# Two halves of 512 tokens as two streams in a kernel with two attention branches and two layers

## The chip, the cores and the metric

The kernel runs on one core of one Trainium2 chip. The metric is the device time of one launch in microseconds; lower is better. PE is TensorE (matmuls; PEld is its weight loads), DVE is VectorE, ACT is ScalarE, POOL is GpSimd and SP is SyncE, which here issues the DMAs inside the loop. Each engine works through its own list of instructions in the order in which it is written; engines meet only at semaphores.

## What is computed

For each of four batch elements (1024 tokens of 128 features) the input is normalised and given to two branches whose results are added to the input. The first branch, called the group branch here, is one transformer layer with 16 heads of 8 features, 4 key heads and a causal window of 32 tokens. The second is two layers with 8 heads of 64 features and local attention over blocks of 64 tokens.

```python
x = L0_attn_x
xn = _layernorm(x, axis=-1)
x = x + _L0_attn_ref(xn, ...) + _L0_ffn_ref(xn, ...)

# one of the two layers of _L0_ffn_ref
h = shift_token(x)                  # half of the features come from the token before
q, k, v = split(h @ wqkv)
q, k = l2norm(q) * qs, l2norm(k) * ksc
q, k = rotary_xpos(q, k)
o = local_attention(q, k, v)        # block of 64 queries, its block and the one before; masked softmax
x = x + o @ wo
h = shift_token(x)
h = (h - mu) / sqrt(var + 1e-05) * lg + lb
a, g = split(h @ w1 + b1)
x = x + (a * gelu(g)) @ w2 + b2
```

## The kernel before

The four batch elements run one after the other in a loop with a barrier between two. Within one, tokens are handled in two halves of 512 (`c` is 0 or 1, `CH` is 512) and eight tiles of 128 (`t`); data lies with features on partitions and tokens along the row. All is float32. Every engine's order is written out by hand.

The order of one element is: transposes in, projections and attention of the group branch, its output; then for each layer `l` of the second branch the projections of half 0, the projections of half 1, local attention of all eight tiles, and output projection and feed-forward of both halves; then the transposes out. The group branch's own feed-forward (`a_hidden`, `a_output`) stands among the feed-forward of the layers.

*Products* go through a ring of four banks of PSUM: `product(i, ...)` writes bank `i % RING`, where `i` is a use numbered by the table `STAGES`; `taken` waits until a use has been drained.

*A projection tile* (`k` from 0 to 7; four of keys, four of queries) is one product on PE; two copies on ACT out of its bank, `raw` (scaled, L976) and `sq` (squared, L980); two DMAs that SP issues (L452) to write `rot`, which is `raw` with neighbouring rows exchanged; on DVE `pc` = `raw` x table (L1038) and `ps_` = `rot` x table (L1040); and on POOL their sum into `qk` (L494). There are four slots of `raw` and `rot`. The sums of squares (L739), turned by PE, become norms by a chain of small operations on DVE (`norms`, L292 to L1179), which PE turns and spreads (`turn_norms`, L755, `spread_norms`) and DVE multiplies into the key tiles (`scale`, L1188). Values (`vB`, L995) are also needed shifted by 64 tokens: two large DMAs per half write `vS` (L460, L462), issued by SP behind the last exchange of the half.

*Local attention* of a tile has two groups `g` of four heads. PE puts the mask into two banks (L620) and adds 16 products of queries and keys (L628), in which the groups, and with them the upper and lower 64 rows, alternate; DVE takes the maximum of both groups (L1085) and multiplies by the norm (L1087); ACT takes eight exponentials with their sums (L872, each with a read of the accumulator); DVE inverts the sums (L1101, L1107) and scales group 0 (L1103), POOL group 1 (L500); PE turns (L640); DVE copies group 0 to `probT` (L1094) and ACT group 1 (L883); PE weighs the values (L656); ACT copies the heads to `oT` (L889). Scores have two pairs of banks, turned probabilities one bank for each group, heads two banks. The loop runs one tile ahead with scores, one behind with the turn and two behind with the weighing.

*Feed-forward* of a half: output projection (four products into one bank), sum and shift on DVE (L1209, L1131, L1132), centring and mean by products, copies on ACT (L914, L915), the root as Exp(-0.5 x Ln) on ACT (L921, L926), their product on DVE (`hTz<-raw,ps_`, L1127), six hidden products, Gelu on ACT (L1013), the gate on DVE (L1235), three products out and the sum (L1243). On ACT, Ln, Exp and Gelu each need a table load when the one before was another.

## Time and profile before

| | before |
|---|---|
| median of 3 runs | 1451.54 us (1446.1 to 1462.14) |
| profiled execution, its own time | 1459.8 us |
| its span, first to last instruction | 1458.1 us |
| mean granted TensorE clock | 0.877 |
| busy: PE, DVE, ACT, POOL | 77%, 60%, 53%, 20% |

Shares are of the span. The granted clock is a share of full speed: 1.00 is 2.4 GHz and 0.50 is 1.2 GHz, and the rows show no third level. In a timeline row, the number in brackets is how long the engine had been idle before, and what ended that.

### The profile page before, as it was taken

Reading aid. Unit: us, or ns where it says so; the run is one execution under the profiler, and the core shown is the slowest. Engines: PE = TensorE matmul, PEld = TensorE weight load, DVE = VectorE, ACT = ScalarE, POOL = GpSimd, SP = SyncE. Lnnn points to the kernel's source line nnn. Section 1 sums busy time; section 2 is a strip of 40 time slices with the busy share of each in tenths; the row PEclk is TensorE's granted clock in tenths of the full one; section 3 lists DMA queues with packets and bytes.
Section 4 is the critical chain, followed back from the end, with each engine's and each line's share of the span. In section 5 each row is a group of like instructions: output and inputs, shape, how many; then the busy total and the mean of one; then the engine's idle time right before and its main releaser. Section 6 shows DMA issues by size and latency. Waiting matters only on the chain. (4 is left out here: it accounts for less than half of the span.)

```text
span 1458.1 us, 23509 instructions
## 1 busy us (share of the span) xinstructions
PE 1124.0 (77%) x8682; PEld 620.1 (43%) x8754; DVE 878.6 (60%) x1738; ACT 768.9 (53%) x1928; POOL 291.5 (20%) x228
## 2 busy tenths in 40 slices
PE   5986788678698668867869877886787976797677
PEld 4752453154374245325437425432534732542353
DVE  5549655963445865596345596468545467648744
ACT  1355674485235556447523556653942453945574
POOL 1105112410101411241010141033202033204210
PEclk9698899889859879988986988997997796999799
DMA  6003101400101310140010131023001014003100
GB/s 260 1 29 117 27 1 58 112 2 15 31 1 45 101 27 1 58 112 2 15 32 1 51 98 23 1 73 98 2 15 32 1 59 111 2 1 123 48 16 15
DMA packets 39201, 66.22 MB, mean 45 GB/s; under 512 B 5408, under 2 KB 19232, under 8 KB 37152
## 3 DMA queue, kind: packets, MB, share of 16 engines
q1 hardware_dynamic: 37920, 62.43, 14.0%
q10 hardware_dynamic: 1152, 2.10, 0.4%
q8 instruction: 78, 1.28, 0.4%
q14 instruction: 51, 0.42, 0.1%
HBM read 13.12 MB, written 2.10 MB: 10 GB/s over the span
## 5 line engine op out<-in xcount | busy, mean ns | idle before, releaser
L494 POOL TENSOR_TENSOR qk<-pc,ps_ 128x512 f32<-128x512 f32 x128 | 194.3, 1518 | 583.8 <-DVE ps_ L1040 583.8
L872 ACT ACTIVATE prob<-bank,negb,inv_norm 128x128 f32<-128x128 f32 x512 | 233.0, 580 | 57.3 <-DVE negb L1087 57.3
L1040 DVE TENSOR_TENSOR ps_<-rot,tab_s 128x512 f32<-128x512 f32 x128 | 172.5, 1347 | 25.9 <-DMA rot<-raw 25.9
L872 ACT ACTIVATION_READ_ACCUMULATOR prob<-bank,negb,inv_norm 128x1 f32 x512 | 163.3, 328 | 0.0
L510 PE MATMUL bank<-hTz,wb_s 128*128 128x512 f32 x256 | 139.5, 675 | 4.3 <-ACT sq L980 4.3
L1085 DVE TENSOR_REDUCE negb<-bank 128x8 f32<-128x1024 f32 x64 | 78.3, 1223 | 94.5 <-PE bank L628 94.4
L976 ACT ACTIVATE raw<-bank,vec_s 128x512 f32<-128x512 f32 x128 | 90.0, 703 | 81.6 <-PE bank L510 46.5
L500 POOL TENSOR_TENSOR prob<-prob,recb 128x512 f32<-128x512 f32 x64 | 66.7, 1041 | 320.1 <-DVE recb L1107 320.1
L1038 DVE TENSOR_TENSOR pc<-raw,tab_s 128x512 f32<-128x512 f32 x128 | 109.3, 854 | 18.2 <-ACT raw L976 18.1
L656 PE MATMUL bank<-probT,vS 128*64 128x64 f32 x1024 | 67.9, 231 | 38.6 <-issue 34.2
L510 PE MATMUL bank<-hTz,w_s 128*128 128x512 f32 (+1 forms) x192 | 87.8, 602 | 12.2 <-DVE hTz L1127 12.2
L620 PE MATMUL bank<-cbf_s 128*128 128x512 bf16 x80 | 35.7, 485 | 71.8 <-ACT prob L872 56.0
L980 ACT ACTIVATE sq<-bank 128x512 f32<-128x512 f32 x128 | 77.8, 608 | 24.1 <-PE bank L739 24.1
L536 PEld LDWEIGHTS bank<-kD,qZ 32*128 32x128 f32 x1024 | 81.7, 245 | 20.2 <-issue 20.2
L841 ACT ACTIVATE a_probT<-bank 128x512 f32<-128x512 f32 x64 | 38.1, 596 | 92.9 <-PE bank L547 92.9
L536 PE MATMUL bank<-kD,qZ 32*128 32x64 f32 (+1 forms) x1024 | 86.9, 335 | 0.0
L628 PE MATMUL bank<-qk 64*64 64x128 f32 (+1 forms) x2048 | 86.5, 311 | 0.0
L628 PEld LDWEIGHTS bank<-qk 64*64 64x64 f32 x2048 | 68.5, 158 | 37.0 <-issue 37.0
L1051 DVE TENSOR_REDUCE a_max<-bank 128x8 f32<-128x512 f32 x64 | 43.9, 686 | 64.5 <-PE bank L536 64.5
L510 PE MATMUL bank<-wb_s,hTz 128*128 128x512 f32 x128 | 75.6, 693 | 3.6 <-ACT sq L980 3.4
L510 PEld LDWEIGHTS bank<-hTz,wb_s 128*128 128x128 f32 x256 | 49.5, 208 | 65.6 <-issue 58.0
L656 PEld LDWEIGHTS bank<-probT,vS 128*64 128x64 f32 x1024 | 55.7, 140 | 50.8 <-issue 42.9
(151 smaller groups left out, 2020.8 us busy)
## 6 DMA issues: line engine op xcount, KB each, us to landing
rot<-raw SPq DMA_DIRECT2D x256, 128.0 KB, 2.0
vS<-vB SPq DMA_DIRECT2D x24, 512.0 KB, 4.4
vS<-vB SPq DMA_DIRECT2D x8, 384.0 KB, 5.7
xn_tok<-x SPq DMA_DIRECT2D x5, 512.0 KB, 3.6
tab_s<-tabs SPq DMA_DIRECT2D x1, 2048.0 KB, 21.0
vS<-x SPq DMA_DIRECT2D x4, 512.0 KB, 3.7
out<-vS SPq DMA_DIRECT2D x8, 256.0 KB, 2.4
wb_s<-wb SPq DMA_DIRECT2D x1, 1536.0 KB, 16.6
```

Of the source, the lines that this page charges most:

```text
L494: pool.tensor_tensor(dst, pc[:, j % 2, :], ps_[:, j % 2, :], ALU.add).then_inc(sum_rdy, 1)
L500: pool.tensor_tensor(p, p, wide(recb[:, t % 2, 1, :]), ALU.mult).then_inc(win_norm[1], 1)
L510: mm = pe.matmul(bank[0:m, i % RING, 0:n], lhs, rhs, start=(q == 0), stop=(q == len(parts) - 1))
L536: mm = pe.matmul(bank[:, m % 4, n0:(w + 1) * 2 * A_WIN], qZ[r, q0 // A_WIN, :, :].rearrange("p j q -> p (j q)"), kD[r, k0:q0 + A_WIN], sta ...
L628: mm = pe.matmul(dst[64 * half:64 * half + 64, g, (h + 1) * P - w:(h + 1) * P], qk[r, h, q0:q0 + 64], qk[r, 4 + h, q0 + 64 - w:q0 + 64], s ...
L656: mm = pe.matmul(head_bank[t % 2][64 * g:64 * g + 64, h * P + 64 * half:h * P + 64 * half + 64], v, probT[:, t % 2, g, h, 64 * half:64 * h ...
L872: ins = act.activation(prob[:, t % 2, g, h, :], s_bank[t % 2][:, g, h * P:(h + 1) * P], ACT.Exp, bias=negb[:, t % 2, g, h:h + 1], scale=qu ...
L976: act.activation(raw[:, jb % 4, :], bank[:, i % RING, :], ACT.Identity, scale=vec_s[:, g:g + 1]).then_inc(raw_rdy, 1)
L980: act.activation(sq[:, jb % 4, :], bank[:, i % RING, :], ACT.Square)\
L1038: dve.tensor_tensor(pc[:, j % 2, :], raw[:, jb % 4, :], ct, ALU.mult)
L1040: dve.tensor_tensor(ps_[:, j % 2, :], rot[:, jb % 4, :], st, ALU.mult).then_inc(prod_rdy, 1)
L1085: link(dve.tensor_reduce(b_, s_bank[t % 2].rearrange("p g (h k) -> p g h k", h=4), AX_X, ALU.max, negate=True))
```

## The change

All of it lies in the second branch and in the numbering of bank uses; what is computed stays. Attention is cut into units: one group of four heads of one tile. `step(l, c, i)` on each engine does what is due at step `i` of the eight units of a half: PE scores unit `i`, weighs a tile at even `i`, turns unit `i-2`; DVE takes the maximum of unit `i`, scales unit `i-1` and may copy unit `i-2`; ACT takes the exponentials of unit `i`, may copy unit `i-2`, and copies heads out.

The steps of half 0 are written among the projections of half 1 of the same layer (`AFTER_TILE`, `AFTER_VALUES`). The steps of half 1 are written among the output projection and feed-forward of half 0. In layer 0 the feed-forward of half 1, with the group branch's, is written among the projections of half 0 of layer 1; in layer 1 it stands alone, behind it only the transposes out.

To have banks for both streams the ring shrinks from four to three, one bank (`SIDE`) holds sums of squares and norms, each group's scores have one bank, and turned probabilities and heads one bank in all; so `window_turn` waits for the copy of the unit before, and `window_weigh` for `oT` of the tile before. `raw` and `rot` have three slots for four. `prob` has three buffers of one unit. The copies to `probT` are all ACT's in half 0 and all DVE's in half 1. The DMAs of `vS` are issued per tile, two behind each of the first four exchanges of half 1 and the rest behind the last.

```diff
-RING = 4
...
+RING = 3
+SIDE = 3
+SLOTS = 3
+
+AFTER_TILE = {3: (0,), 4: (1,), 5: (2, 3), 6: (4,), 7: (5,)}
+AFTER_VALUES = {0: (6,), 1: (7,), 2: (8,), 3: (9,)}
+LAY_VECTOR = ((False, False), (True, True))
...
+        raw = sb("raw", [P, SLOTS, CH])
+        rot = sb("rot", [P, SLOTS, CH])
+        prob = sb("prob", [P, 3, 4, P])
+        probT = sb("probT", [P, 2, 4, P])
...
-        s_bank = [bank[:, 0:2, :], bank[:, 2:4, :]]
+        w_score, w_turn, w_head = (bank[:, 4, :], bank[:, 5, :]), bank[:, 6, :], bank[:, 7, :]
...
+                        if c:
+                            for t in range(TPC, TILES) if k == B_QK - 1 else (k,) if k < TPC else ():
+                                taken(sp, USE["v", l, t])
+                                if t == TPC:
+                                    sp.wait_ge(sums_turned, l * CHUNKS + 2)
+                                if l:
+                                    sp.wait_ge(win_heads, on(l, 0))
+                                sp.dma_start(vS[64:128, t, :], vB[0:64, t, :]).then_inc(v_shifted[t], 16)
+                                if t + 1 < TILES:
+                                    sp.dma_start(vS[0:64, t + 1, :], vB[64:128, t, :]).then_inc(v_shifted[t + 1], 16)
...
+                    def window_scores(l, c, i):
+
+                        n = unit(l, c, i)
+                        t, g = c * TPC + i // 2, i % 2
+                        if n >= 2:
+                            pe.wait_ge(win_exp, n - 1)
+                        if i == 0:
...
+                        pe.matmul(w_score[g], identb, wmask[t == 0], start=True, stop=False, skip_group_check=True)
+                        r = slice(64 * g, 64 * g + 64)
...
+                                mm = pe.matmul(w_score[g][64 * half:64 * half + 64, (h + 1) * P - w:(h + 1) * P],
+                                               qk[r, h, q0:q0 + 64], qk[r, 4 + h, q0 + 64 - w:q0 + 64],
+                                               start=False, stop=(h == 3), skip_group_check=True)
...
+                        if on(l, t):
+                            pe.wait_ge(on_rdy, on(l, t))
...
+                    def step(l, c, i):
+
+                        if i < 2 * TPC:
+                            window_scores(l, c, i)
+                        if i >= 4 and i % 2 == 0:
+                            window_weigh(l, c * TPC + (i - 4) // 2)
+                        if 2 <= i < 2 * TPC + 2:
+                            window_turn(l, c, i - 2)
...
+                        for k in range(B_QK):
+                            project(l, 1, k)
+                            if k == 2:
+                                turn_norms(l, 0)
+                                spread_norms(l, 0, (0, 1))
+                            if k == 3:
+                                spread_norms(l, 0, (2, 3))
+                            if k == 5:
+                                sum_squares(l, 1, 0)
+                            for i in AFTER_TILE.get(k, ()):
+                                step(l, 0, i)
...
+                        step(l, 0, 10)
+
+                        step(l, 1, 0)
+                        step(l, 1, 1)
+                        head_sum(l, 0)
+                        step(l, 1, 2)
+                        step(l, 1, 3)
+                        centre(l, 0)
+                        step(l, 1, 4)
+                        mean(l, 0)
+                        for i in (5, 6, 7):
+                            step(l, 1, i)
+                        mlp_hidden(l, 0)
+                        step(l, 1, 8)
+                        step(l, 1, 9)
+                        mlp_output(l, 0)
+                        step(l, 1, 10)
+
+                        if l == 0:
+                            head_sum(0, 1)
+                            project(1, 0, 0)
+                            project(1, 0, 1)
+                            centre(0, 1)
+                            project(1, 0, 2)
+                            project(1, 0, 3)
+                            mean(0, 1)
+                            project(1, 0, 4)
+                            project(1, 0, 5)
+                            sum_squares(1, 0, 0)
+                            for f in range(4):
+                                a_hidden(0, f)
+                            project(1, 0, 6)
+                            project(1, 0, 7)
+                            mlp_hidden(0, 1)
+                            value(1, 0)
+                            sum_squares(1, 0, 1)
+                            value(1, 1)
+                            turn_sums(1, 0)
+                            a_output(0)
+                            mlp_output(0, 1)
+                            value(1, 2)
+                            value(1, 3)
+                    head_sum(1, 1)
+                    a_hidden(1, 0)
+                    a_hidden(1, 1)
+                    centre(1, 1)
+                    a_hidden(1, 2)
+                    a_hidden(1, 3)
+                    to_tokens(0)
+                    mean(1, 1)
+                    a_output(1)
+                    mlp_hidden(1, 1)
+                    mlp_output(1, 1)
+                    to_tokens(1)
...
+                    def step(l, c, i):
+
+                        if i < 2 * TPC:
+                            window_probs(l, c, i)
+                        if 2 <= i < 2 * TPC + 2 and not LAY_VECTOR[c][i % 2]:
+                            lay(act, l, c, i - 2)
+                        if i >= 5 and i % 2:
+                            window_out(l, c * TPC + (i - 5) // 2)
...
+                        for k in range(B_QK):
+                            project(l, 1, k)
+                            if k == 2:
+                                copy_norms(l, 0)
+                            for i in AFTER_TILE.get(k, ()):
+                                step(l, 0, i)
+                        for tt in range(TPC):
+                            if tt == 0:
+                                copy_sums(l, 1)
+                            value(l, TPC + tt)
+                            for i in AFTER_VALUES[tt]:
+                                step(l, 0, i)
+                        copy_norms(l, 1)
+                        step(l, 0, 11)
+
+                        for i in range(4):
+                            step(l, 1, i)
+                        centred(l, 0)
+                        step(l, 1, 4)
+                        step(l, 1, 5)
+                        log(l, 0)
+                        root(l, 0)
+                        step(l, 1, 6)
+                        step(l, 1, 7)
+                        gelus(l, 0)
+                        for i in (8, 9, 11):
+                            step(l, 1, i)
+
+                        if l == 0:
+                            project(1, 0, 0)
+                            project(1, 0, 1)
+                            centred(0, 1)
+                            project(1, 0, 2)
+                            project(1, 0, 3)
+                            log(0, 1)
+                            root(0, 1)
+                            project(1, 0, 4)
+                            project(1, 0, 5)
+                            for f in range(4):
+                                a_hidden(0, f)
+                            project(1, 0, 6)
+                            project(1, 0, 7)
+                            gelus(0, 1)
+                            copy_sums(1, 0)
+                            for t in range(TPC):
+                                value(1, t)
...
+                    def step(l, c, i):
+
+                        if i < 2 * TPC:
+                            window_maxima(l, c, i)
+                        if 1 <= i <= 2 * TPC:
+                            window_scale(l, c, i - 1)
+                        if 2 <= i < 2 * TPC + 2 and LAY_VECTOR[c][i % 2]:
+                            lay(dve, l, c, i - 2)
...
+                        norms(l, 0)
+                        for k in range(B_QK):
+                            turn_pairs(l, 1, k)
+                            if k == 2:
+                                scale(l, 0, (0, 1))
+                            if k == 3:
+                                scale(l, 0, (2, 3))
+                            for i in AFTER_TILE.get(k, ()):
+                                step(l, 0, i)
+                        step(l, 0, 6)
+                        step(l, 0, 7)
+                        norms(l, 1)
+                        step(l, 0, 8)
+                        step(l, 0, 9)
+                        for k in range(4, B_QK):
+                            dve.wait_ge(sum_rdy, pair(l, 1, k) + 1)
+                        scale(l, 1, range(4))
+
+                        step(l, 1, 0)
+                        step(l, 1, 1)
+                        head_sum(l, 0)
+                        for i in range(2, 6):
+                            step(l, 1, i)
+                        normed(l, 0)
+                        step(l, 1, 6)
+                        step(l, 1, 7)
+                        gated(l, 0)
+                        step(l, 1, 8)
+                        step(l, 1, 9)
+                        mlp_sum(l, 0)
+
+                        if l == 0:
+                            head_sum(0, 1)
+                            for k in range(4):
+                                turn_pairs(1, 0, k)
+                            normed(0, 1)
+                            for k in range(4, B_QK):
+                                turn_pairs(1, 0, k)
+                            gated(0, 1)
+                            a_output(0)
+                            mlp_sum(0, 1)
+                    head_sum(1, 1)
+                    dve.wait_ge(next_in, 16)
+                    norm_tokens(dve, link)
+                    dve.wait_ge(x_in, 16)
+                    to_tokens(0)
+                    a_output(1)
+                    normed(1, 1)
+                    keep_moments(dve, link)
+                    gated(1, 1)
+                    mlp_sum(1, 1)
+                    to_tokens(1)
 
```

On ACT, at the second half's projections of layer 0 (`raw` and `sq` belong to a projection tile, `prob` are exponentials), before:

```order
L980 ACTIVATE sq<-bank 128x512 [waits squares_summed]
L965 ACTIVATE rT<-bank 24x512 [waits norms_turned]
L976 ACTIVATE raw<-bank,vec_s 128x512 [waits rotary_products,product_ready]
L980 ACTIVATE sq<-bank 128x512 [waits squares_summed]
L976 ACTIVATE raw<-bank,vec_s 128x512 [waits rotary_products,product_ready]
L980 ACTIVATE sq<-bank 128x512 [waits squares_summed]
L976 ACTIVATE raw<-bank,vec_s 128x512 [waits rotary_products,product_ready]
```

and now, from the fourth tile on:

```order
L1036 ACTIVATE raw<-bank,vec_s 128x512 [waits rotary_products,product_ready]
L1040 ACTIVATE sq<-bank 128x512 [waits squares_summed]
L981 ACTIVATE prob,sumb<-bank,negb,inv_norm 128x128 [waits window_maxima_ready]
L981 ACTIVATE prob,sumb<-bank,negb,inv_norm 128x128 x3
L1036 ACTIVATE raw<-bank,vec_s 128x512 [waits rotary_products,product_ready]
L1040 ACTIVATE sq<-bank 128x512 [waits squares_summed]
L981 ACTIVATE prob,sumb<-bank,negb,inv_norm 128x128 [waits window_maxima_ready]
L981 ACTIVATE prob,sumb<-bank,negb,inv_norm 128x128 x3
L1036 ACTIVATE raw<-bank,vec_s 128x512 [waits rotary_products,product_ready]
L1040 ACTIVATE sq<-bank 128x512 [waits squares_summed]
```

The exponentials, which stood behind all projections and value copies, stand between the two copies of one tile and those of the next: four for each unit.

On DVE at the same place (`pc` and `ps_` rotate a projection tile, `qk<-bank,qk` is a scaling by norms, `negb` a maximum), before:

```order
L1188 TENSOR_TENSOR qk<-bank,qk 128x512 [waits product_ready,rotated]
L1038 TENSOR_TENSOR pc<-raw,tab_s 128x512 [waits raw_copied,rotated]
L1040 TENSOR_TENSOR ps_<-rot,tab_s 128x512 [waits rows_exchanged0]
L1188 TENSOR_TENSOR qk<-bank,qk 128x512 [waits product_ready,rotated]
L1038 TENSOR_TENSOR pc<-raw,tab_s 128x512 [waits raw_copied,rotated]
L1040 TENSOR_TENSOR ps_<-rot,tab_s 128x512 [waits rows_exchanged1]
L1188 TENSOR_TENSOR qk<-bank,qk 128x512 [waits product_ready,rotated]
```

and now, from the fifth tile on:

```order
L1184 TENSOR_TENSOR pc<-raw,tab_s 128x512 [waits raw_copied,rotated]
L1186 TENSOR_TENSOR ps_<-rot,tab_s 128x512 [waits rows_exchanged0]
L1230 TENSOR_REDUCE negb<-bank 128x4 [waits window_scores_ready]
L1232 TENSOR_TENSOR negb<-negb,inv_norm 128x4 [waits vector_step]
L1241 RECIPROCAL recb<-sumb 128x4 [waits window_probs_ready]
L1243 TENSOR_TENSOR prob<-prob,recb 128x512 [waits vector_step]
L1184 TENSOR_TENSOR pc<-raw,tab_s 128x512 [waits raw_copied,rotated]
L1186 TENSOR_TENSOR ps_<-rot,tab_s 128x512 [waits rows_exchanged1]
L1230 TENSOR_REDUCE negb<-bank 128x4 [waits window_scores_ready]
```

Behind each rotation now stand the maximum of a unit and the scaling of the unit before it; the scalings by norms moved ahead, behind the third and the fourth tile.

## Rows read from the trace of the kernel before

**Rows 1.** The list of cores: microseconds of the span, mean granted TensorE clock.

```profile
core 0: 1458.1 us, clock 0.877
```

**Rows 2.** The page's part 1: busy us, share of the span, instructions.

```profile
PE 1124.0 (77%) x8682; PEld 620.1 (43%) x8754; DVE 878.6 (60%) x1738; ACT 768.9 (53%) x1928; POOL 291.5 (20%) x228
```

**Rows 3.** Windows of one steady batch element: stretch, us, busy per engine, PEclk, DMA.

```profile
386.30:751.80 365.50, 282.28 (x2159) 156.68 (x2177) 216.17 (x413) 192.27 (x483) 72.66 (x55) 0.85 0.13 39
386.30:486.10 99.80, 87.80 (x663) 56.61 (x670) 56.62 (x84) 45.55 (x81) 18.40 (x12) 0.77 0.08 28
486.10:521.50 35.40, 21.00 (x61) 6.65 (x61) 28.03 (x55) 13.48 (x24) 11.29 (x8) 0.79 0.42 115
521.50:567.70 46.20, 33.72 (x587) 26.62 (x592) 23.82 (x48) 35.94 (x143) 8.33 (x8) 0.86 0.01 2
567.70:604.70 37.00, 33.64 (x77) 13.79 (x77) 17.39 (x53) 16.90 (x23) 0.00 (x0) 1.00 0.00 1
604.70:622.10 17.40, 15.47 (x46) 5.51 (x45) 15.26 (x17) 11.33 (x20) 9.06 (x6) 1.00 0.33 121
703.90:741.00 37.10, 33.73 (x79) 13.80 (x78) 15.34 (x46) 16.90 (x23) 0.00 (x0) 1.00 0.05 15
741.00:751.80 10.80, 1.27 (x10) 0.79 (x8) 3.47 (x7) 1.25 (x1) 2.21 (x3) 0.75 0.19 53
```

**Rows 4.** Timeline of layer 1's first projections: start us, us, engine, instruction [idle before].

```profile
605.79 0.69 ACT L976 ACTIVATE raw<-bank,vec_s 128x512 f32<-128x512 f32 x1 [4.81 <-PE bank L510]
...
609.13 0.69 DVE L1040 TENSOR_TENSOR ps_<-rot,tab_s 128x512 f32<-128x512 f32 x1 [1.84 <-DMA rot<-raw]
...
612.64 1.75 DVE L1040 TENSOR_TENSOR ps_<-rot,tab_s 128x512 f32<-128x512 f32 x1
...
614.92 1.75 DVE L1040 TENSOR_TENSOR ps_<-rot,tab_s 128x512 f32<-128x512 f32 x1
```

**Rows 5.** Timeline of the start of local attention, layer 0.

```profile
521.78 0.63 PE L620 MATMUL bank<-cbf_s 128*128 128x512 bf16 x1 [1.87 <-DVE qk L1188]
...
522.34 1.99 PE L628 MATMUL bank<-qk 64*64 64x64 f32 x32
...
524.38 1.22 DVE L1085 TENSOR_REDUCE negb<-bank 128x8 f32<-128x1024 f32 x1 [3.12 <-PE bank L628]
...
525.63 0.17 DVE L1087 TENSOR_TENSOR negb<-negb,inv_norm 128x8 f32<-128x8 f32 x1
...
525.84 0.46 ACT L872 ACTIVATE prob<-bank,negb,inv_norm 128x128 f32<-128x128 f32 x1 [7.87 <-DVE negb L1087]
...
527.60 0.46 ACT L872 ACTIVATE prob<-bank,negb,inv_norm 128x128 f32<-128x128 f32 x1
```

**Rows 6.** Timeline of a steady tile of local attention.

```profile
535.04 1.10 PE L628 MATMUL bank<-qk 64*64 64x128 f32 x32
...
538.39 0.63 ACT L889 ACTIVATE oT<-bank 128x512 f32<-128x512 f32 x1
...
539.35 0.51 ACT L872 ACTIVATE prob<-bank,negb,inv_norm 128x128 f32<-128x128 f32 x1
```

**Rows 7.** Groups of instructions by form: busy us, mean ns of one | idle before.

```profile
L510 PE MATMUL bank<-oT,wob_s 128*128 128x512 f32 x128 | 57.1, 599 | 0.0
...
L1051 DVE TENSOR_REDUCE a_max<-bank 128x8 f32<-128x512 f32 x64 | 43.9, 686 | 64.5 <-PE bank L536 64.5
...
L1235 DVE SCALAR_TENSOR_TENSOR oT<-bank,bias,vS 128x512 f32<-128x512 f32 x32 | 24.0, 751 | 41.9 <-ACT vS L1013 41.9
...
L921 ACT ACT_TABLE_LOAD x12 | 15.4, 1283 | 0.2
```

**Rows 8.** Timeline of the second half's norms, layer 0.

```profile
512.00 0.21 DVE L292 TENSOR_SCALAR nw<-bank 128x64 f32<-128x64 f32 x1
...
516.75 0.60 PE L755 MATMUL bank<-cbf_s,rsp 128*24 128x128 bf16 x4 [4.72 <-DVE rsp L1179]
...
518.77 2.48 DVE L1188 TENSOR_TENSOR qk<-bank,qk 128x512 f32<-128x512 f32 x4 [2.07 <-PE bank L510]
```

863 lines of the change are left out of this document (393 added, 470 removed).

## The prediction

> **What bounds the kernel now.** I read the page's head first: the span is 1458.1 us, PE is busy 77% of it, and the granted clock of PE is 0.877 on the mean [rows 1, 2]. No engine is near its limit throughout, so the bound has to be read stage by stage. The windows of one steady batch element do that [rows 3]. It takes 365.5 us: 99.8 us up to the end of the first half's projections, then, in layer 0, 35.4 us for the projections of the second half, 46.2 us of local attention, 37.0 us of output projection and feed-forward, and 17.4 us of the first half's projections of layer 1. Layer 1 repeats the projections and the attention (81.8 us: 365.5 less the other seven windows, 283.7) and ends with 37.1 + 10.8 us. The reader is to see three different limits. In the 35.4 us DVE is busy 28.0: it is the bound, with PE at 21.0. In the 46.2 us ACT is busy 35.9. In the 37.0 us PE is busy 33.6 at a granted clock of 1.00. That is what the change can use: ACT-bound attention beside DVE-bound projections, and beside PE-bound feed-forward.
>
> Then the timelines, for what one step costs when it waits. A projection passes ACT (raw), a DMA that exchanges rows, and DVE (ps_): raw starts at 605.79 and ps_ at 609.13, DVE having been idle 1.84 for the DMA [rows 4]. So **raw start to ps_ start is 3.34 us**. Before, this shows only once per run of projections: later ps_ start 2.28 us apart (612.64, 614.92 [rows 4]), since ACT runs ahead. At the start of attention, PE's mask begins at 521.78, DVE's maximum at 524.38, ACT's first exponential at 525.84 and the fifth at 527.60 [rows 5]: **four heads cost ACT 1.76 us**. In the steady state ACT bounds a tile: between 538.39 and 539.35 it makes two copies, 0.48 each [rows 6], and eight exponentials are 3.5, together 4.5.
>
> **The change, part by part.** Work is nearly constant; the order is what changes. Call the new stretches of a layer A (second half's projections with the first half's attention), B (second half's attention with the first half's feed-forward) and C (second half's feed-forward with the first half's projections of layer 1; in layer 1 a tail instead).
>
> *A, the loop.* In ACT's new order the exponentials of a unit (four heads) stand between raw of one projection and raw of the next, and in DVE's the maximum of that unit stands behind ps_. The exponentials wait for the maximum, the maximum stands behind ps_, ps_ waits for the DMA, the DMA for raw. ACT can no longer run ahead, so the exchange's latency is paid for each tile. One turn is 3.34 + 0.69 (ps_ at 609.13 [rows 4]) + 0.05 + 0.93 (maximum of one bank 0.69 [rows 7], its product with the norm 0.17 [rows 5], handoffs 0.07) + 1.76 = **6.8 us**, where a projection took 2.3 before. From raw of tile 4 to the end of unit 5 there are four turns, one more unit (its maximum hidden, 1.75) and five copies on ACT at 0.48: 27.1 + 1.8 + 2.4 = 31.3.
>
> *A, head and end.* Ahead of the loop: the norms (4.75 from 512.00 to 516.75 [rows 8]; take 4), four rotations at 2.3, four scalings at 0.62 [rows 8], less 0.7 that overlaps: 15. SP's queue changes here: the large vS transfers no longer stand ahead of the first exchange, but two small ones stand behind each of the first four; I cost that at nothing, since DVE's 2.3 a tile covers it (an issue is an SP instruction of some 0.5 to 0.6, four a tile; if they don't fit, 0.1 to 0.5 a tile, 2 at most in A). Then the first scores (2.6 for both groups at half clock [rows 5]; 2.3 for one), maximum 0.9 and exponentials 1.8: raw of tile 4 at 20. Loop: 51.3. Behind it little is beside anything: units 6 and 7 with their value copies (6.0: with one head bank each weighing waits for the copy before it), the norms of the second half (4), the last unit's reciprocal, POOL product and turn (2.4), and what ran from 516.75 to 521.78 (5.0 [rows 5, 8]): 68.7. PE is sparse here, as in the 35.4 us with a granted clock of 0.79 [rows 3]; for half clock on the sums of squares and scores that DVE waits for I add 1.3. **A = 70.** Before, projections and half the attention took 35.4 + 23.1 = 58.5.
>
> *B.* Per unit DVE does a maximum (0.93), a copy to probT (0.69, as one bank's maximum) and each other time a scaling (0.9): 2.1 us on the mean against ACT's 1.8. Around them DVE stands in order behind the other stream. It waits for scores (2.3), then for the output projection, four products (two records of 0.60 each, overlapping [rows 7]) and the start at half clock: at 11 the shifted sum is done. Units 2 to 5 run to 22.4. Then normed waits for Ln and Exp with two table loads of 1.28 each [rows 7]: with the copy before them 4.3 that nothing hides, as the next maximum is queued behind normed on DVE: 27.4. Units 6 and 7 to 31. Gelu with a table load and six products through a ring of three banks, then gated, three times 0.75 [rows 7]: 37.7. Two turned copies, three products and the sum with its shift: **B = 44.** Before: the other branch's hidden and output products are some 7.4 of the 37.0 (eight products of about 0.93), so half of attention and half of the rest are 23.1 + 14.8 = 37.9. Here too the latencies are added, not hidden.
>
> *C.* About 34 us of PE work. DVE's shift at 5.4, eight rotations of 2.3, gated, then a_output (four products), mlp_output (three) and the shift in a row: **C = 38**, against 14.8 + 7.4 + 17.4 = 39.6. The tail in layer 1: 14.8 + 7.4, 2 for DVE's statistics of the next element, which now stand ahead of gated, and the 10.8 behind the last product: **35**, against 47.9 for both halves.
>
> *Costed at nothing:* three raw slots for four (raw of tile k waits for ps_ of k-3, which ends 5.1 ahead of ps_ of k at a pitch of 2.28, and needs 3.34); the ring of three in the front part, where DVE's 2.28 a tile hides it; the table loads in C and the tail, where ACT waits for products. Without that cover each load is 1.28, 5 us in four elements.
>
> **Sum.** Layer 0: 70 + 44 + 38 = 152 for 136.0. Layer 1: 70 + 44 + 35 = 149 for 129.7. Together 301 + 99.8 = 400.8 for 365.5: +35.3 per element, +141 in four. The profiled execution, 1459.8 us with a span of 1458.1, stands 0.6% above the median of the runs, 1451.5. Against that median: 1451.5 + 141 = **1593 us**, 10% slower.
>
> **PE's scores, bounded.** Scores of a tile alternated between two row halves: 32 matmul records in 1.10 us at full clock [rows 6], 1.99 at half clock [rows 5]. Now a unit keeps to one row half, and no row shows that. Bounds: 0.55 (nothing lost) and 2.2 (no two overlap any more). I take 1.05, half lost, since column halves still alternate. The high end is 1.15 more for each of some seven units a layer on the path: 8 us, 65 in all. The Trainium skill ("TensorE: Matmul & The Clock Gate", Part 3, The mechanism) says that a weight load overlaps running matmuls only when its row group differs, which speaks against this change; by that rule the high end would hold, and the sum would be about 1658.
>
> **Rivals.**
> *The streams overlap as meant* (faster): A falls to DVE's work, 28.0 + 11.9 [rows 3] plus 5 of fill, 45; B and C to PE's work, 35 and 36. Layers of 116 and 113, element 329, 1451.5 - 4 x 36.5 = **1306**. Its place is the loop in A: it decides once a turn takes under 3.5 us, which needs ACT ahead of DVE, and ACT's order does not let it. For it: no engine is busy over 80% in the 35.4 us. Chance 0.10.
> *No change*: the loop is as I say, but A's end and B overlap better (A 62, B 36): element 368.8, **1465**. Chance 0.06.
> *Scores in series*, as bounded above: **1658**. Chance 0.12.
> *Half clock*: PE waits more often, and its terms on the path (4.7 in A's end, 10 to 15 in B) double: up to 20 a layer, 160 in all, **1753**. For it: the 35.4 us had 0.79. Against it: attention had 0.86 with as many waits [rows 3]. Chance 0.12.
> *Forecast*: 0.60, own range 1510 to 1680.
>
> **Range and chances.** 1490 to 1720 leaves out the first two and the worst of half clock, 0.2 in all. Faster by over 1% (under 1437; 1% is about what a measurement here can tell from no change) 0.11, within 1% 0.05, slower 0.84.
>
> **What would show it.** In A, ps_ 6.5 to 7.5 us apart from tile 4 on, or more, each after an idle stretch of DVE that the rot DMA ended, and ACT idle before exponentials for DVE's negb; A 65 to 75. In B, DVE idle for about 4 us before hTz<-raw,ps_, ended by ACT. Mean clock below 0.877. I am wrong if ps_ in A stay within 4 us of each other, or if DVE or PE is busy over 85% in A; the size is wrong if B ends near 36.

## The result, and the profile after

| | before | after |
|---|---|---|
| median | 1450.22 us (1446.1 to 1462.14) | 1658.56 us (1647.59 to 1668.58) |
| ratio to before, 95% interval | | 1.142, 1.132 to 1.152 |
| profiled execution, span | 1458.1 us | 1645.9 us |
| mean granted clock | 0.877 | 0.830 |
| busy: PE, DVE, ACT, POOL | 77%, 60%, 53%, 20% | 77%, 52%, 48%, 17% |

The change makes the kernel 14% slower: 208 us by the medians, 188 us by the two profiled spans. 1593 us was forecast, with a range of 1490 to 1720.

The list of cores and part 1 of the page, which answer [rows 1, 2] (span, clock; busy us, share, instructions):

```profile
core 0: 1645.9 us, clock 0.830
```

```profile
PE 1274.4 (77%) x8754; PEld 696.9 (42%) x8754; DVE 858.3 (52%) x1874; ACT 791.7 (48%) x1944; POOL 286.2 (17%) x228
```

The work of DVE, ACT and POOL is what it was, within 3%. PE's grew by 150 us on the same products: more of it runs at half clock, and the scores take longer.

The windows of the second batch element, which answer [rows 3] (stretch, us, busy of PE, PEld, DVE, ACT, POOL, granted clock, DMA share, GB/s). In order: the element, its front part, then A, B and C of layer 0, A and B of layer 1, the tail:

```profile
434.20:836.50 402.30, 312.50 (x2177) 169.75 (x2177) 210.70 (x447) 197.67 (x487) 71.34 (x55) 0.83 0.12 36
434.20:524.85 90.65, 80.32 (x669) 49.74 (x670) 57.11 (x86) 45.43 (x82) 18.34 (x12) 0.88 0.09 30
524.85:595.76 70.91, 46.93 (x356) 25.13 (x354) 34.28 (x81) 33.34 (x100) 15.07 (x12) 0.76 0.21 58
595.76:638.29 42.53, 36.33 (x327) 22.12 (x327) 21.56 (x47) 25.17 (x79) 4.17 (x4) 0.88 0.01 1
638.29:682.09 43.80, 39.30 (x94) 14.31 (x95) 24.24 (x33) 22.43 (x36) 12.35 (x8) 0.92 0.13 48
682.09:754.60 72.51, 48.32 (x355) 26.02 (x353) 33.23 (x77) 34.01 (x100) 15.05 (x12) 0.73 0.21 57
754.60:801.70 47.10, 39.43 (x326) 23.32 (x325) 21.33 (x46) 25.40 (x79) 4.17 (x4) 0.83 0.00 1
801.70:836.50 34.80, 21.89 (x55) 9.12 (x55) 18.95 (x79) 11.88 (x15) 2.21 (x3) 0.89 0.11 32
```

In A no engine is busy much: DVE 34.3 of 70.9 us, ACT 33.3, PE 46.9 at a clock of 0.76. Two streams run there, and both wait.

Means over the whole execution (four elements, eight layers), each stretch measured between the same instructions in both kernels. For the kernel before, A and B are taken as forecast: its projections plus half its attention, and the other half plus its share of feed-forward.

| us | forecast | after | before |
|---|---|---|---|
| element | 400.8 | 404.6 | 357.8 |
| front part | 99.8 | 94.9 | 96.8 |
| A, a layer | 70 | 72.6 | 57.5 |
| B, a layer | 44 | 43.9 | 37.0 |
| C | 38 | 42.7 | 39.6 |
| tail | 35 | 33.9 | 32.1 |

So of 46.8 us more in an element, A gives 30 (15.1 twice), B 14 (6.9 twice), C 3, the tail 2, and the front part takes 2 back.

The loop in A, timeline of the changed kernel (start, us, engine, instruction, idle before it and what ended that):

```profile
551.44 0.70 ACT L1036 ACTIVATE raw<-bank,vec_s 128x512 f32<-128x512 f32 x1
...
554.77 0.69 DVE L1186 TENSOR_TENSOR ps_<-rot,tab_s 128x512 f32<-128x512 f32 x1 [1.84 <-DMA rot<-raw]
...
556.10 0.73 DVE L1232 TENSOR_TENSOR negb<-negb,inv_norm 128x4 f32<-128x4 f32 x1
...
556.86 0.46 ACT L981 ACTIVATE prob<-bank,negb,inv_norm 128x128 f32<-128x128 f32 x1 [4.24 <-DVE negb L1232]
...
559.37 1.09 PE L687 MATMUL bank<-ident_s,prob 128*128 128x128 f32 x4 [6.34 <-ACT probT L466]
...
562.20 0.69 ACT L1036 ACTIVATE raw<-bank,vec_s 128x512 f32<-128x512 f32 x1 [0.73 <-PE bank L558]
...
565.48 0.69 DVE L1186 TENSOR_TENSOR ps_<-rot,tab_s 128x512 f32<-128x512 f32 x1 [1.80 <-DMA rot<-raw]
...
573.15 0.69 DVE L1186 TENSOR_TENSOR ps_<-rot,tab_s 128x512 f32<-128x512 f32 x1 [1.85 <-DMA rot<-raw]
...
577.49 0.17 DVE L1232 TENSOR_TENSOR negb<-negb,inv_norm 128x4 f32<-128x4 f32 x1
```

The reader sees the turn as it was described: raw at 551.44, ps_ at 554.77 after an idle stretch that the row exchange ended, the exponentials at 556.86. Of the three intervals of ps_ from tile 4 on (547.15, 554.77, 565.48, 573.15) two are single turns, 7.6 and 7.7 us. The one with two units in it is 10.7 us, and in it PE stands 6.34 us before a turn, for ACT's copy out of the one bank of turned probabilities, with the product of the next projection queued behind that turn. Most of the 6.34 is the same chain once more, since the copy stands behind the exponentials that wait for negb; what the bank adds, and the prediction did not have, is the 0.73 for which raw at 562.20 waits for its product.

The wait in B, same view:

```profile
615.92 1.28 ACT L1013 ACT_TABLE_LOAD   x1
...
617.92 1.28 ACT L1020 ACT_TABLE_LOAD   x1
...
619.95 0.69 DVE L1263 TENSOR_TENSOR hTz<-raw,ps_ 128x512 f32<-128x512 f32 x1 [5.02 <-ACT ps_ L1020]
```

The scores, from part 5 of the page (busy us, mean ns of one) and from the timeline at full clock:

```profile
L674 PE MATMUL bank<-qk 64*64 64x128 f32 (+1 forms) x2048 | 167.0, 305 | 0.0
```

```profile
551.93 1.09 PE L674 MATMUL bank<-qk 64*64 64x128 f32 x16
```

16 records take what 32 took in [rows 6].

### The profile page after: what moved, and what is told of

Same layout as the page of the kernel before. It is cut to its first block and busy times, and to the rows that moved or that the text cites. A ratio compares the mean times of both kernels' runs of the same rounds, so it can differ in the third digit from the quotient of the medians.

```text
span 1645.9 us, 23837 instructions
## 1 busy us (share of the span) xinstructions
PE 1274.4 (77%) x8754; PEld 696.9 (42%) x8754; DVE 858.3 (52%) x1874; ACT 791.7 (48%) x1944; POOL 286.2 (17%) x228
## 3 DMA queue, kind: packets, MB, share of 16 engines
q8 instruction: 78, 1.28, 0.3%
## 5 line engine op out<-in xcount | busy, mean ns | idle before, releaser
L1186 DVE TENSOR_TENSOR ps_<-rot,tab_s 128x512 f32<-128x512 f32 x128 | 138.4, 1082 | 109.7 <-DMA rot<-raw 109.2
L687 PE MATMUL bank<-ident_s,prob 128*128 128x128 f32 x512 | 101.9, 332 | 104.9 <-ACT probT L466 73.0
L674 PE MATMUL bank<-qk 64*64 64x128 f32 (+1 forms) x2048 | 167.0, 305 | 0.0
L674 PEld LDWEIGHTS bank<-qk 64*64 64x64 f32 x2048 | 131.8, 155 | 68.7 <-issue 68.7
L1184 DVE TENSOR_TENSOR pc<-raw,tab_s 128x512 f32<-128x512 f32 x128 | 93.0, 726 | 112.1 <-ACT raw L1036 111.8
L1230 DVE TENSOR_REDUCE negb<-bank 128x4 f32<-128x512 f32 x128 | 87.7, 685 | 116.9 <-PE bank L674 116.7
L687 PEld LDWEIGHTS bank<-ident_s,prob 128*128 128x128 f32 x512 | 66.5, 165 | 131.5 <-issue 86.4
L981 ACT ACTIVATION_READ_ACCUMULATOR prob<-bank,negb,inv_norm 128x1 f32 x512 | 106.4, 208 | 0.0
L989 ACT ACTIVATE oT<-bank 128x512 f32<-128x512 f32 x64 | 38.6, 604 | 90.7 <-PE bank L702 90.7
L668 PE MATMUL bank<-cbf_s 128*128 128x512 bf16 x128 | 59.5, 465 | 22.0 <-POOL qk L524 16.4
## 6 DMA issues: line engine op xcount, KB each, us to landing
tab_s<-tabs SPq DMA_DIRECT2D x1, 2048.0 KB, 21.2
```

Of the source, the lines that this page charges most:

```text
L674: mm = pe.matmul(w_score[g][64 * half:64 * half + 64, (h + 1) * P - w:(h + 1) * P], qk[r, h, q0:q0 + 64], qk[r, 4 + h, q0 + 64 - w:q0 + 64 ...
L687: mm = pe.transpose(w_turn[:, h * P:(h + 1) * P], prob[:, n % 3, h, :], ident_s[:, :])
L981: ins = act.activation(prob[:, n % 3, h, :], w_score[g][:, h * P:(h + 1) * P], ACT.Exp, bias=negb[:, t % 2, g, h:h + 1], scale=query_norm( ...
L1184: dve.tensor_tensor(pc[:, j % 2, :], raw[:, jb % SLOTS, :], ct, ALU.mult)
L1186: dve.tensor_tensor(ps_[:, j % 2, :], rot[:, jb % SLOTS, :], st, ALU.mult)\
L1230: link(dve.tensor_reduce(b_, w_score[g].rearrange("p (h k) -> p h k", h=4), AX_X, ALU.max, negate=True))
```

## The experiments

Twelve kernels, each against the kernel before on the same chip:

| kernel | built on | median us | ratio to before | 95% interval |
|---|---|---|---|---|
| after | | 1658.6 | 1.142 | 1.132 to 1.152 |
| a_apart | after | 1581.1 | 1.090 | 1.082 to 1.099 |
| a_ahead | after | 1604.7 | 1.108 | 1.099 to 1.117 |
| ahead_lay | a_ahead | 1582.8 | 1.090 | 1.084 to 1.096 |
| b_apart | after | 1766.4 | 1.219 | 1.211 to 1.228 |
| no_ln | after | 1630.5 | 1.123 | 1.115 to 1.130 |
| late_add | after | 1656.9 | 1.133 | 1.122 to 1.144 |
| apart_best | a_apart | 1584.2 | 1.092 | 1.086 to 1.098 |
| one_half | before | 1487.9 | 1.017 | 1.008 to 1.026 |
| one_turn | before | 1496.2 | 1.029 | 1.022 to 1.036 |
| two_banks | before | 1798.0 | 1.227 | 1.216 to 1.239 |
| two_busy | two_banks | 1669.5 | 1.150 | 1.144 to 1.156 |
| b_both | before | 1428.9 | 0.977 | 0.968 to 0.986 |

Means by stretch in the profiled execution, for the kernels that have streams:

| us | element | front | A | B | C | tail |
|---|---|---|---|---|---|---|
| after | 404.6 | 94.9 | 72.6 | 43.9 | 42.7 | 33.9 |
| a_apart | 386.2 | 92.2 | 64.3 | 44.5 | 42.6 | 33.8 |
| a_ahead | 394.4 | 96.4 | 65.6 | 45.1 | 42.6 | 33.9 |
| ahead_lay | 386.8 | 92.6 | 63.4 | 45.3 | 42.8 | 34.0 |
| b_apart | 433.9 | 92.7 | 72.8 | 60.9 | 40.1 | 33.7 |
| no_ln | 401.9 | 93.9 | 73.5 | 43.2 | 40.5 | 34.0 |
| late_add | 406.9 | 96.4 | 72.5 | 44.4 | 42.7 | 33.9 |
| apart_best | 388.7 | 93.0 | 65.2 | 44.0 | 43.3 | 33.9 |

The front part is the same work in all of them and moves by 4 us, so a difference under 1 us in A or B says nothing. The ratios of one_half, two_banks, late_add and b_both go by seven runs of the kernel before that spread from 1449.7 to 1487.1 us; by the lowest four of the seven they would be 1.021, 1.235, 1.139 and 0.981.

### Is it the order in A? a_apart, a_ahead, ahead_lay

```diff
-AFTER_TILE = {3: (0,), 4: (1,), 5: (2, 3), 6: (4,), 7: (5,)}
-AFTER_VALUES = {0: (6,), 1: (7,), 2: (8,), 3: (9,)}
+AFTER_TILE = {}
+AFTER_VALUES = {0: (), 1: (), 2: (), 3: tuple(range(10))}
```

> The changed kernel with one part undone: in A the steps of the first half's attention stand behind all projections and value copies of the second half, on every engine; banks, units and slots stay those of the changed kernel, and B and C are as they were. Theory (the order makes the loss): in the changed kernel's trace a turn of A's loop takes 7.6 us (ps_ starts 547.15 and 554.77), because the exponentials stand between two projections on ScalarE. Without that, projections run at 2.3 us again and the units at about 3.0 us: 28 us to the end of the value copies, 8 x 3.0 = 24 for the units, 16 for the norms of the second half and the last tile. A falls from 73.5 to about 68, the kernel to about 1600 us, although nothing overlaps any more. Rival (units, single banks for turned probabilities and heads, and three slots make the loss, and the interleaving itself helps): the units keep their 7 us or so, and without the projections beside them A grows to 80 or more: 1700 us.

A fell from 72.6 to 64.3, more than expected, and the kernel to 1581 us. So the interleaving in A costs 8.3 us a layer: running the two streams one behind the other is faster. That is the theory's sign. But 64.3 is still 6.8 above the 57.5 of the kernel before, and no projection stands among the units any more.

```diff
+AHEAD_TILE = {4: (0,), 5: (1,), 6: (2, 3), 7: (4,)}
+AHEAD_VALUES = {0: (5, 6), 1: (7,), 2: (8,), 3: (9,)}
@@ TensorE and ScalarE, second half's projections
-                            for i in AFTER_TILE.get(k, ()):
+                            for i in AHEAD_TILE.get(k, ()):
```

> The changed kernel with one difference: on TensorE and ScalarE a projection of the second half is written ahead of the step that stood before it (steps behind tiles 4, 5, 6, 7 instead of 3, 4, 5, 6, 7), VectorE and GpSimd keep their order. The work is the same. Theory (one turn is raw, row exchange by DMA, ps_, maximum, exponentials in a row): the exchange of the next tile now runs beside the maximum and the exponentials, so a turn falls from 7.6 us to what ScalarE and VectorE do in it: two copies 1.07, four exponentials 1.76, one or two copies of 0.48 each against pc, ps_ (1.2), maximum and product 1.4, reciprocal and scaling 0.9: about 4 us. Four to five turns a layer, 13 us a layer, 104 us in eight layers: about 1542 us, with ps_ about 4 us apart and no idle time of VectorE ended by the rot DMA. Rival (TensorE's scores in one row half, 1.09 to 1.97 us a unit, or the half clock set the pitch): ps_ stay 7 us apart and the time within 1% of 1650.

A fell by 7.0, where 13 was expected, and the span by 41 us, not 104. Timeline of a_ahead:

```profile
540.18 0.68 DVE L1188 TENSOR_TENSOR ps_<-rot,tab_s 128x512 f32<-128x512 f32 x1
...
542.32 0.60 ACT L1042 ACTIVATE sq<-bank 128x512 f32<-128x512 f32 x1 [5.42 <-PE bank L761]
...
547.91 0.69 DVE L1188 TENSOR_TENSOR ps_<-rot,tab_s 128x512 f32<-128x512 f32 x1 [1.69 <-DMA rot<-raw]
...
552.49 1.09 PE L689 MATMUL bank<-ident_s,prob 128*128 128x128 f32 x4 [3.52 <-ACT probT L468]
...
553.31 0.68 DVE L1188 TENSOR_TENSOR ps_<-rot,tab_s 128x512 f32<-128x512 f32 x1
...
559.33 0.69 DVE L1188 TENSOR_TENSOR ps_<-rot,tab_s 128x512 f32<-128x512 f32 x1 [1.08 <-DMA rot<-raw]
```

ps_ are 7.7, 5.4 and 6.0 us apart, not 4. The exchange is off the chain in the second interval, as the theory says. What holds the others is PE: ACT's square waits 5.42 us for the sums of squares, since `sq` has four slots and PE sums the first four only behind the sixth projection, and PE waits 3.52 for the copy out of the one bank of turned probabilities. With one in-order queue per engine, the chain that was taken away was only the longest of three.

```diff
@@ ScalarE, step
-                        if i < 2 * TPC:
-                            window_probs(l, c, i)
                         if 2 <= i < 2 * TPC + 2 and not LAY_VECTOR[c][i % 2]:
                             lay(act, l, c, i - 2)
+                        if i < 2 * TPC:
+                            window_probs(l, c, i)
```

> The kernel a_ahead with one difference: in a step of the first half's attention ScalarE's copy of the turned probabilities stands ahead of the four exponentials, not behind them. In a_ahead's trace TensorE stands idle 3.52 us at 552.49 for that copy (turned probabilities have one bank), with the next projection queued behind the turn. Theory (with the exchange off the chain, the one bank of turned probabilities sets the pitch): the copy comes 1.8 us or more earlier, 3 us a layer at the two double steps and some 1 us behind the projections, -30 us: about 1575. Rival (the turn's place in TensorE's order doesn't matter, the copy only delays the exponentials by 0.5 each): 1605 or above.

1583 us for 1605, and A 63.4 for 65.6, which is 18 us in eight layers; the front part, where nothing was changed, is 3.8 us an element shorter, 15 of the 30 us between the two spans. So the bank of turned probabilities was the next limit in A, and worth 18 of the 30 us that were expected. Even so A is no better than in a_apart, where nothing overlaps.

### Is B no better? b_apart

```diff
@@ TensorE (ScalarE and VectorE alike)
-                        step(l, 1, 0)
-                        step(l, 1, 1)
-                        head_sum(l, 0)
...
+                        for i in range(11):
+                            step(l, 1, i)
+                        head_sum(l, 0)
+                        centre(l, 0)
+                        mean(l, 0)
+                        mlp_hidden(l, 0)
+                        mlp_output(l, 0)
```

> The changed kernel with B undone: the second half's attention first, all of it, then the output projection and feed-forward of the first half; A and C are as in the changed kernel. Theory (B hides part of the latencies, but pays about what it hides): attention alone 8 units of 2.6 us and 8 us for start and end, 29; output projection and feed-forward of one half alone about 21 (the chain product 1.9, sum and shift 1.5, centring 1.0, copies 1.1, mean 1.0, two table loads 2.56 with Ln and Exp 1.3, hTz 0.7, six products 5, gate 0.8, three products 1.5, sum and shift 1.6, handoffs 3). 50 us for 43.1 now: +55 us in eight layers, about 1705 us. Rival (interleaving in B hides nothing, its waits cost as much as they save): within 1% of 1650.

B rose from 43.9 to 60.9: interleaving saves 17.0 us a layer there, two and a half times the 6.9 that the theory had left it (C gives 2.6 back). Windows of b_apart, the second half's attention and then the first half's output projection and feed-forward:

```profile
631.17:666.00 34.83, 26.99 (x296) 20.50 (x296) 15.68 (x36) 16.57 (x68) 4.16 (x4) 0.76 0.01 2
666.00:690.33 24.33, 16.93 (x33) 6.26 (x31) 4.54 (x8) 8.90 (x11) 0.00 (x0) 0.79 0.00 0
```

This is the most telling pair of lines of the study. Half of the attention, with nothing beside it, takes 34.8 us; in the kernel before the whole takes 46.2, so half of it 23.1 [rows 3]. ACT has no more to do (16.57 against half of 35.94), but that fills 48% of the stretch, not 78%. And the feed-forward of one half alone takes 24.3, where both together, with 7.4 of the group branch's by the prediction's estimate, took 37.0 [rows 3]. **The loss is in the pieces before any two of them are interleaved.** Its timeline:

```profile
639.43 1.97 PE L674 MATMUL bank<-qk 64*64 64x128 f32 x16
```

```profile
639.00 0.46 ACT L973 ACTIVATE prob<-bank,negb,inv_norm 128x128 f32<-128x128 f32 x1 [1.78 <-DVE negb L1218]
...
642.38 0.46 ACT L973 ACTIVATE prob<-bank,negb,inv_norm 128x128 f32<-128x128 f32 x1 [1.51 <-DVE negb L1218]
```

A unit takes 3.4 us here, and each time ACT waits for a maximum, which waits for scores at half clock. Over the whole stretch the eight units' first exponentials (633.59 to 657.07) are 3.35 apart on the mean, where the kernel before needs 4.44 for a tile of two units. The other 11.4 of the 34.8 us are start and end; the kernel before pays about as much once a layer, this one once a half.

Taken together, if the two edits add (they were not made in one kernel): with both streams apart a layer takes 64.3 + 60.9 = 125.2 in A and B, against 57.5 + 37.0 = 94.5 in the kernel before. Splitting the work into single halves, units and fewer banks costs 30.7 us a layer; interleaving returns 17.0 in B and takes 8.3 in A. 30.7 - 17.0 + 8.3 = 22.0, which is 72.6 + 43.9 less 94.5. How the 30.7 divides among the second start and end of attention, the order of the scores, the banks and the slots was not separated; the runs below bound two of the parts.

### What do the pieces lack? one_half, one_turn, two_banks, two_busy

Here the kernel before gets one restriction of the changed kernel at a time.

```diff
-                        for h in range(4):
-                            for half in range(2):
-                                for g in range(2):
+                        for g in range(2):
+                            for h in range(4):
+                                for half in range(2):
```

> The kernel before with one difference: the 32 score products of a tile are written group by group, so 16 in a row keep to one row half, as in the changed kernel, where in the kernel before they alternate. Banks and waits stay. The changed kernel's trace shows 1.09 us for 16 records so (2.2 a tile), against 1.10 for 32. Theory (scores in one row half cost, but are a small part of the loss): in the steady tile of 4.5 us ScalarE is busy all the time and TensorE about 3.8; with 1.1 more TensorE becomes the limit, 4.9 to 5.2 a tile. 64 tiles by 0.4 to 0.7 and the first tile of each layer: +45 us, about 1495. Rival (ScalarE hides it): within 1% of 1450. Rival (it is the main cost of the change): more than 1.1 us a tile, 1520 and above.

1.7% slower. Attention went from 44.4 to 47.5 us a layer. The 32 records of a tile take 1.59 us here, not the 2.2 that the changed kernel's units let expect (timeline):

```profile
539.09 1.59 PE L628 MATMUL bank<-qk 64*64 64x128 f32 x32
```

But PE does not become the limit of a steady tile: from the fourth tile on, exponentials of one tile and the next start 4.44 us apart in both kernels, so ScalarE hides it there. The cost lies at the start, where PE runs at half clock and ACT has nothing to do yet (timeline; before, the same 32 records took 1.99 [rows 5]):

```profile
520.50 2.89 PE L628 MATMUL bank<-qk 64*64 64x64 f32 x32
```

On the mean of eight layers the first exponential comes 4.40 us behind the first score, for 3.50; the second tile follows the first by 3.80, for 3.50, and the third the second by 6.15, for 5.10. It is a real cost and a small one; the rival that made it the main cost is out. In the changed kernel attention starts twice a layer.

```diff
@@ window_turn: both groups into one bank
-                            if on(l, t):
-                                pe.wait_ge(win_laid[g], on(l, t))
+                            if g:
+                                pe.wait_ge(win_laid[0], on(l, t) + 1)
+                            elif on(l, t):
+                                pe.wait_ge(win_laid[1], on(l, t))
@@ window_weigh: heads into one bank
-                        if on(l, t) >= 2:
-                            pe.wait_ge(on_rdy, on(l, t) - 1)
+                        if on(l, t):
+                            pe.wait_ge(on_rdy, on(l, t))
```

> The kernel before with the turned probabilities of both groups in one bank and the heads in one bank, as in the changed kernel; scores keep their two pairs. The turn of group 1 waits for VectorE's copy of group 0, and each weighing for the copy of the heads before it. Theory (score banks are what matters, these two cost little): TensorE has mask 0.6, scores 1.1, weighing 1.1 and two turns of 0.55 in a tile, 3.9, and now waits 0.9 between the turns for a copy of 0.69 and its handoffs: 4.8 against ScalarE's 4.5. 64 tiles by 0.3 to 0.5: +25 us, about 1477. Rival (any bank less breaks the overlap as in two_banks): over 1600.

2.9% slower, attention 48.5 us a layer, with 4.64 a steady tile for 4.44. The wait is where it was expected (timeline):

```profile
543.88 0.63 PE L642 MATMUL bank<-ident_s,prob 128*128 128x128 f32 x4 [0.88 <-DVE probT L1096]
```

Together the two restrictions are 7 us a layer of the 30.7, if they add.

```diff
-        s_bank = [bank[:, 0:2, :], bank[:, 2:4, :]]
+        s_bank = [bank[:, 0:2, :], bank[:, 0:2, :]]
@@ window_scores, with the order of one_half
+                            if t:
+                                pe.wait_ge(win_exp, 2 * on(l, t - 1) + g + 1)
```

> The kernel before with one_half's order of scores and, besides, one pair of score banks for two: the scores of a group wait for that group's exponentials of the tile before. That is what the changed kernel has, where each group has one bank. Theory (what the streams had to give up in banks costs more than their order): behind the last exponential there is nothing left to do for ScalarE but two copies of 0.48 while the chain mask 0.3, scores 1.1, maximum 1.23, product 0.17 and handoffs 0.15 runs, 2.95 in all. A tile takes 3.5 + 2.95 = 6.4 us for 4.5, 64 times: +125 us, about 1575. Rival (banks are not what is short; the changed kernel loses by its order of projections alone): within 1% of one_half.

23% slower, 339 us by the medians, where 125 was expected: attention takes 86.9 us a layer for 44.4, a tile 10.9. Timeline and window of the attention:

```profile
642.81 0.61 PE L620 MATMUL bank<-cbf_s 128*128 128x512 bf16 x1 [2.45 <-ACT prob L871]
643.35 1.97 PE L627 MATMUL bank<-qk 64*64 64x128 f32 x16
...
645.79 1.97 PE L627 MATMUL bank<-qk 64*64 64x128 f32 x16
```

```profile
647.81 1.23 DVE L1084 TENSOR_REDUCE negb<-bank 128x8 f32<-128x1024 f32 x1 [6.68 <-PE bank L627]
```

```profile
605.70:693.68 87.98, 65.19 (x592) 50.05 (x591) 23.60 (x48) 37.13 (x143) 8.32 (x8) 0.60 0.00 1
```

The sum had taken the masks and scores at full clock and left out that ACT's copy stands ahead of its exponentials and waits for weighing and turns: with the next scores no longer ahead, masks, scores, weighing, turns, copy and exponentials are one chain, most of it at 1.2 GHz (granted clock 0.60). two_banks is harsher than the changed kernel (it waits by tiles with the maximum over both groups), so it shows what kind of cost this is, not its size there.

```diff
@@ window_scores of two_banks
+                        if t:
+                            for _ in range(2):
+                                pe.matmul(bank[:, 3, :], ones_s[:, :], hT[:, 0:CH], start=True, stop=True,
+                                          skip_group_check=True)
```

> The kernel two_banks with two products of 128x512 more for each tile but the first, written into a bank that is free there, ahead of TensorE's wait for the exponentials; nothing reads them. Work is added, none taken away. In two_banks' trace attention takes 86.9 us a layer, with the granted clock at 0.50 and TensorE idle 2.45 us ahead of the mask. Theory (a good part of two_banks' loss is the half clock, not the missing bank): with TensorE busy through the wait the clock is at 1.00, scores take 2.2 us for 3.9, masks 0.6 for 1.2, turn 1.1 for 2.0, weighing 1.1 for 1.9: a tile falls from 10.8 to about 7.3 us, 3.5 x 7 x 8 = 196 us, about 1600. Rival (the waits alone make it, or the clock stays low): 1800 or above, since each product takes 0.9 to 1.9 us and the wait is only 2.45.

With 112 products more, 129 us less: 1669.5 against 1798.0. Attention is 71.9 us a layer. Window and timeline of two_busy:

```profile
572.20:643.37 71.17, 58.45 (x614) 40.77 (x620) 23.62 (x48) 37.13 (x143) 8.32 (x8) 0.86 0.01 1
```

```profile
598.82 1.88 PE L619 MATMUL bank<-hTz,ones_s 128*128 128x512 f32 x4
601.75 1.09 PE L631 MATMUL bank<-qk 64*64 64x128 f32 x16 [1.05 <-ACT prob L875]
```

A tile at full clock takes 7.7 us (scores at 594.03 and 601.75), about as expected; the clock does not stay up throughout (0.86), which is why less than 196 us came. So over a third of two_banks' loss (129 of 339 us) is half clock that its waits bring with them; the rest is the waits, and the half clock that stays.

### Two terms of the sum: late_add, no_ln

```diff
@@ GpSimd, rotated, from the fifth tile of the second half on
+                        if n:
+                            pool.wait_ge(win_max, n)
```

> The changed kernel with one wait more: in A, from the fifth tile on, GpSimd's sum of pc and ps_ starts behind the product of the maximum with the norm and not directly behind ps_. Work and orders are the same. In the changed kernel's trace that product of VectorE (128x4) takes 0.73 us where GpSimd's sum (1.27 us) runs and 0.17 us where it does not (548.48 and 577.49). Theory (VectorE's operation with two inputs from SBUF is held while GpSimd's runs, so the held time is part of the turn): the product is back at 0.17, a turn 0.56 us shorter, four or five turns a layer: 8 x 2.5 = 20 us, about 1637. Rival (the long record is an effect of what stands next to it on VectorE): the product stays at 0.73 and the time at 1650 or above.

1657 us: nothing gained, though the cause of the long product was the right one. Timeline of late_add, VectorE and then GpSimd:

```profile
558.00 0.69 DVE L1188 TENSOR_TENSOR ps_<-rot,tab_s 128x512 f32<-128x512 f32 x1 [1.84 <-DMA rot<-raw]
...
559.32 0.17 DVE L1234 TENSOR_TENSOR negb<-negb,inv_norm 128x4 f32<-128x4 f32 x1
```

```profile
560.49 1.26 POOL L526 TENSOR_TENSOR qk<-pc,ps_ 128x512 f32<-128x512 f32 x1 [6.89 <-DVE negb L1234]
561.71 1.51 POOL L535 TENSOR_TENSOR prob<-prob,recb 128x512 f32<-128x512 f32 x1
```

The product is back at 0.17 us. But GpSimd's scaling of group 1, queued behind its sum, now ends 5.2 us behind ps_, in the changed kernel 3.3 (557.00 + 1.04 behind 554.77), and with it the turn, the product queued behind the turn and the next raw: the interval with two units in it is 12.3 us for 10.7 (ps_ at 558.0 and 570.3). A wait was moved onto another engine's queue.

```diff
-                        act.activation(ln_buffers(l, c)[2], bank[:, i % RING, :], ACT.Ln,
+                        act.activation(ln_buffers(l, c)[2], bank[:, i % RING, :], ACT.Square,
```

> The changed kernel with the logarithm of the variance replaced by a square on ScalarE, so part of the computation is left out and the values are others: Ln needs a table of its own, Square none. In B that takes away both table loads ahead of hTz<-raw,ps_ (1.28 us each), in C and the tail one of three loads a layer. Theory of the prediction (loads cost in B alone, and are hidden in C and in the tail): B 2.6 us shorter, C and tail the same, 8 x 2.6 = 20 us, about 1630 us. Rival (loads are on the path in C and in the tail too, since ring banks stay taken behind them): another 1.3 us in each, 30 us in all, about 1620 us, and C at 41.4 us instead of 42.7. The windows of the trace tell it, the whole time hardly does.

1631 us: 28 less than the changed kernel by the medians, 11 by the two spans. Timeline of no_ln in B:

```profile
624.74 0.69 DVE L1263 TENSOR_TENSOR hTz<-raw,ps_ 128x512 f32<-128x512 f32 x1 [2.32 <-ACT ps_ L1020]
...
628.14 0.69 DVE L1230 TENSOR_REDUCE negb<-bank 128x4 f32<-128x512 f32 x1 [1.20 <-PE bank L674]
```

The idle time before hTz fell from 5.02 to 2.32, as much as the two loads, but a wait for scores of 1.20 appeared behind it: from the output projection of the first half to that of the second it is 38.9 us for 40.4, 1.5 gained and not 2.6 (0.7 by the table's B, which is within its noise). C, where the loads were called hidden, became 2.2 us shorter, though only one load of 1.28 left it. The tail did not move. So both theories were wrong in part, and the clock has a share in C: it was granted 0.92 there in the changed kernel and 0.96 in no_ln. b_apart, whose C is written the same and has all three loads, ran it at full clock (window of its C):

```profile
690.33:730.40 40.07, 34.92 (x92) 13.08 (x91) 25.69 (x32) 21.83 (x35) 12.36 (x8) 1.00 0.15 53
```

It takes 40.1 us with every load in place, 2.6 less than in the changed kernel, so the 2.2 of no_ln can't be put down to the load alone.

### Could it be mended, and what does the filled stretch hold? apart_best, b_both

> The kernel a_apart with two differences: the copy ahead of the exponentials as in ahead_lay, and VectorE's sum of pc and ps_ as in b_both. The question is whether the stream form of B, with its shared banks, can beat the kernel before when its worst order is mended. Theory (what is left is the price of shared banks, which B's overlap doesn't pay back): the sum gives 0.35 a tile, 32 us, the copy 2 us a layer, 16 us, both from 1581: about 1533, still 5% above the kernel before. Rival (it was the order all along): under 1450.

It has the edit of a_apart, ScalarE's order of ahead_lay and VectorE's sum of b_both (below). 1584 us, the same as a_apart's 1581: the two together brought nothing here, where 48 us were expected, and they were not separated. The copy ahead of the exponentials, which helped in a_ahead, lets ACT wait for PE's turn when nothing stands between (timeline of apart_best):

```profile
545.86 0.60 ACT L466 ACTIVATE probT<-bank 128x512 f32<-128x512 f32 x1 [1.02 <-PE bank L681]
```

No stream kernel came closer to the kernel before than 9%.

```diff
@@ VectorE, rotate (GpSimd's sum is taken out)
                             dve.tensor_tensor(ps_[:, j % 2, :], rot[:, jb % 4, :], st, ALU.mult).then_inc(prod_rdy, 1)
+                            dve.wait_ge(prod_rdy, jb + 1)
...
+                            dve.tensor_tensor(qk[:, qk_tile(k), cc(c)], pc[:, j % 2, :], ps_[:, j % 2, :],
+                                              ALU.add).then_inc(sum_rdy, 1)
@@ SyncE
-                        if jb % B_QK == B_QK - 1:
-                            c = jb // B_QK % CHUNKS
+                        c, k = jb // B_QK % CHUNKS, jb % B_QK
+                        if c and k in (B_QK - 2, B_QK - 1):
+                            c = k - (B_QK - 2)
```

> The kernel before with two differences in its projections, to see whether the stretch that the change set out to fill is short of engines at all. VectorE makes the sum of pc and ps_ itself, in place of GpSimd, and the large vS transfers of the first half are issued behind the seventh exchange of the second half instead of ahead of its first. In the trace of the kernel before ps_ takes 1.75 us beside GpSimd's sum and 0.69 alone, a tile 2.28; the first ps_ of the second half of layer 0 waits 4.09 us for its exchange, which lands behind the vS transfers. Theory: a tile takes three operations of 0.6 and a handoff, 1.9 to 1.95; 0.33 less for 7 tiles of 16 halves is 37 us, and 4 us in layer 0 of each of four elements is 16: about 1398 us. Rival (GpSimd's sum is hidden and the sum on VectorE comes on top): 0.6 more a tile, +65 us, 1500 us.

The only kernel that beats the kernel before: 1428.9 us, 0.977 (0.968 to 0.986). By the medians that is 30 us, by the two spans 43 (the profiled execution was the fastest of its four); 53 were expected. Timeline and window of the second half's projections of layer 0:

```profile
469.91 0.68 DVE L1041 TENSOR_TENSOR ps_<-rot,tab_s 128x512 f32<-128x512 f32 x1
470.63 0.69 DVE L1048 TENSOR_TENSOR qk<-pc,ps_ 128x512 f32<-128x512 f32 x1
...
471.84 0.69 DVE L1041 TENSOR_TENSOR ps_<-rot,tab_s 128x512 f32<-128x512 f32 x1
```

```profile
463.90:493.70 29.80, 20.37 (x62) 6.19 (x60) 24.33 (x52) 12.81 (x23) 0.00 (x0) 0.84 0.50 136
```

ps_ is 0.69 us long and 1.93 apart, for 1.75 and 2.28 before [rows 4], though VectorE does more. Part of what [rows 3] shows as DVE's busy time was time held by GpSimd. The two edits were not run apart; these projections became 5.6 us shorter in layer 0, where the stall behind the vS transfers had been 4.1, and 1.8 in layer 1.

## Why the prediction was right, point by point

**Sign and mechanism.** Slower by over 1% was given 0.84, and the time is inside the forecast's own range. What was to be seen was seen: ps_ apart by 7.6 and 7.7 (6.5 to 7.5 or more was said), each after an idle stretch that the rot DMA ended; ACT idle 4.24 before exponentials for negb; A at 72.6 (65 to 75); DVE idle 5.0 before hTz for ACT (about 4); clock 0.830, below 0.877; DVE and PE busy 48% and 66% in A. "The streams overlap as meant", which needed a turn below 3.5 us, is out.

**The size: 141 us forecast, 188 by spans.** Three errors, in order of size.

*The baseline, 31 us.* The step "this element, 365.5, times four" failed. The element of [rows 3] was the longest of its execution: by the starts of the first transposes the four took 359.2, 365.5, 355.2 and 351.2, mean 357.8. The changed kernel's element was built up mostly from durations of single instructions, so the old side alone was too long, by 7.7 an element, 3.0 of it in the front part.

*A, 2.6 a layer, 21 us.* On the mean of eight layers the head took 19.0 for 20, the loop 33.5 for 31.3 and the end 20.0 for 18.7 (from 18.8 to 21.2, longest where the granted clock was lowest, 0.74 for 0.91). In the loop the turn of 6.8 was 7.7, of which 0.48 is ACT's copy that the sum had apart; the rest is the product of maximum and norm, taken at 0.17 from [rows 5] and 0.73 here, held while GpSimd adds. And the interval with two units was 10.7, where a turn of 7.7, 1.75 and one more copy make 9.9: the rest is raw's wait of 0.73 behind the one bank of turned probabilities. Nothing in the head points at the vS transfers, which were costed at nothing.

*C, 4.7 an element, 19 us.* "Costed at nothing: ... the table loads in C and the tail." Without one of C's three loads C was 2.2 shorter; the tail stayed (no_ln). With all three and the clock at 1.00 for 0.92 it was 2.6 shorter (b_apart). So the sum missed both, and since the loads' waits and the clock go together the two shares were not separated; 40.1 at full clock is still 2 above the 38. PE waits 2.5 us for the gate (667.68) in the changed kernel, with a value product queued on the ring of three, but no run gave the ring its fourth bank back.

Against these, the front part at 94.9 for 99.8, the tail at 33.9 for 35 and B at 43.9 for 44 took 20, 4 and 1 us back; 12 of the 20 are the front part's share of the long element, which stood on both sides of the forecast.

The medians are 20 us further apart than the spans: the profiled execution of after was the fastest of its four, 11 below the median, that of before 10 above its own.

**Reasons that did not hold.** "Here too the latencies are added, not hidden", of B, is wrong as a comparison: b_apart shows interleaving to hide 17.0 us a layer. B is 6.9 longer than before because its two parts had become 23.9 us longer (60.9 for 37.0). The chains that were summed for A and B were the right ones, so their sums came out near; but which property of the change makes them long was named as order, and for the larger part it is the split into single halves and units with half the banks. That the single banks bring half clock with their waits (two_busy) was not in the sum.

**PE's scores.** "I take 1.05": measured 1.09. The high end, no two overlapping, did not come. The Trainium skill ("TensorE: Matmul & The Clock Gate", Part 3, The mechanism), by which a weight load overlaps running matmuls only when its row group differs, has the sign right: one row half takes twice as long. The 1658 us that were worked out with it are the measured median only by accident, since that sum went with 2.2 us a unit.

**Half clock.** The rival's 1753 us did not come, but part of the loss is there: before, the projections stood at 0.79 and attention at 0.86 [rows 3]; A is at 0.76 and 0.73. C was 2.6 us an element shorter where it ran at 1.00 (b_apart). How much of the 208 us it is was not measured; in two_banks it was over a third.

## What to carry to other kernels

Before two streams are interleaved, price each stream alone with the banks and buffers that it will be left with; here that was a loss of 31 us a layer, and the overlap earned back 9. Count how often each stream starts and ends: work that a steady tile hides is not hidden at the start, as one_half shows. An interleave whose engines' queues form a ring (ACT to DMA to DVE to ACT) runs at the ring's latency, and taking one link out exposes the next. And take a baseline from the mean over all repetitions in the trace, not from one window.

## What the runs showed of the hardware

- VectorE's operations with two inputs from SBUF are held while GpSimd works: a 128x4 product takes 0.73 us beside GpSimd's sum and 0.17 without it (late_add), a 128x512 product 1.75 and 0.69. The maximum beside the same sum, read from PSUM, takes 0.68 both times. The Trainium skill ("SBUF — State Buffer", SBUF: two separate sides) says that VectorE with two SBUF inputs and GpSimd take a shared port pair as an exclusive lock for a whole instruction; the trace agrees. With the sum on VectorE itself a projection tile took 1.93 us for 2.28 (b_both).
- Products that nobody reads made a kernel 129 us faster (two_busy against two_banks): TensorE, busy through its wait, was granted 0.86 in the attention for 0.60, 2.4 GHz in place of 1.2 for part of it.
- At full clock 16 score matmuls of one row half alone take 1.09 us, 16 of one and then 16 of the other 1.59 (one_half), and 32 that alternate 1.10 [rows 6]. So the two runs of 16 overlap in part. At half clock the 32 take 2.89 in the first order and 1.99 alternated [rows 5].
